# Delta rule stage: filter taps read PSUM, key norms summed on TensorE, key and output scaling moved to VectorE, the block inverse loaded in two parts, decay masks moved off GpSimd

## The reference

```python
qkvz = x @ W_in                                   # 128 -> 4 * 1024
q, k, v, z = jnp.split(qkvz, 4, axis=-1)
b, a = jnp.split(x @ W_ba, 2, axis=-1)
qkv = silu(causal depthwise convolution of q, k, v with 4 taps)
beta = jax.nn.sigmoid(b)
g = -A * jax.nn.softplus(a + dt_bias)
q = _l2norm(q) * HD ** (-0.5)                     # per head, sum of squares over 64
k = _l2norm(k)
def step(S, inp):                                 # over time, per head
    S = S * jnp.exp(gt)[..., None, None]
    pred = jnp.einsum('bhk,bhkv->bhv', kt, S)
    S = S + jnp.einsum('bhk,bhv->bhkv', kt, (vt - pred) * bt[..., None])
    return S, jnp.einsum('bhk,bhkv->bhv', qt, S)
y = y * jax.lax.rsqrt(jnp.mean(y * y, axis=-1, keepdims=True) + 1e-06)
y = norm_w * y * jax.nn.silu(z)
```

## Time and profile before

| | |
|---|---|
| runs, median of 3 | 5853.05 us |
| profiled execution | 5847.35 us, of it the span 5845.6 us |
| PE busy | 4513.3 us, 77% |
| DVE busy | 3523.2 us, 60% |
| POOL busy | 1876.9 us, 32% |
| ACT busy | 1798.5 us, 31% |
| mean granted TensorE clock | 0.771 |

### The profile page before, as it was taken

The page is one execution under the profiler, slowest core; times in us unless marked ns, Lnnn a source line. Parts: engine busy times, 40 slices in busy tenths (PEclk is TensorE's granted clock), DMA queues, the critical chain, the costliest instruction groups (busy, mean ns, idle before and its releaser), DMA issues. The chain is left out here.

```text
span 5845.6 us, 160862 instructions
## 1 busy us (share of the span) xinstructions
PE 4513.3 (77%) x65093; PEld 3139.4 (54%) x65093; DVE 3523.2 (60%) x6479; ACT 1798.5 (31%) x3215; POOL 1876.9 (32%) x2605
## 2 busy tenths in 40 slices
PE   7888869999664788877888788878788876886544
PEld 6666634444332556655666556656556655665221
DVE  3444458887674666666666666666566543554677
ACT  0000011111343344444444444444444422332000
POOL 1111100000452455555555455554454541000000
PEclk6555579999785888888888888888888885555766
DMA  0000000000463121222222222222222110001110
GB/s 13 11 11 11 12 22 14 11 14 9 108 148 96 37 42 40 43 44 44 42 40 43 42 45 43 41 41 44 43 45 42 41 35 17 18 18 46 30 32 25
DMA packets 702651, 219.50 MB, mean 38 GB/s; under 512 B 561624, under 2 KB 676000, under 8 KB 701600
## 3 DMA queue, kind: packets, MB, share of 16 engines
q1 hardware_dynamic: 693536, 205.97, 15.9%
q10 hardware_dynamic: 8448, 4.20, 0.2%
HBM read 123.44 MB, written 86.53 MB: 36 GB/s over the span
## 5 line engine op out<-in xcount | busy, mean ns | idle before, releaser
L1736 DVE SCALAR_TENSOR_TENSOR d_acc<-d_xr,d_cq,d_acc 128x512 f32<-128x512 f32 x768 | 643.3, 838 | 149.5 <-ACT d_acc L1402 127.9
L1558 PE MATMUL d_pa<-d_wv,d_hs 128*128 128x512 f32 x1024 | 603.5, 743 | 1.1 <-issue 1.0
L1378 POOL TENSOR_TENSOR d_prod<-d_tblk,d_ablk 128x15 f32<-128x15 f32 (+7 forms) x960 | 376.5, 392 | 583.3 <-DMA d_ablk<-a_blocks 513.1
L1533 PE MATMUL d_pa<-d_hq,d_wqk 128*128 128x259 f32 x1024 | 388.6, 515 | 79.7 <-ACT d_acc L1402 50.9
L1381 POOL TENSOR_TENSOR d_tblk<-d_tblk,d_prod 128x15 f32<-128x15 f32 (+7 forms) x960 | 386.9, 403 | 75.2
L1558 PEld LDWEIGHTS d_pa<-d_wv,d_hs 128*128 128x128 f32 x1024 | 248.7, 250 | 284.7 <-issue 269.5
L1596 PE MATMUL d_pb<-d_ti,d_at 32*32 32x16 f32 x8192 | 123.8, 207 | 351.1 <-POOL d_ti L1355 310.6
L1401 ACT ACTIVATE d_xr<-d_pa 128x518 f32<-128x518 f32 x256 | 154.0, 601 | 647.2 <-PE d_pa L1533 644.4
L1596 PEld LDWEIGHTS d_pb<-d_ti,d_at 32*32 32x32 f32 x8192 | 116.7, 147 | 377.2 <-issue 376.9
L1533 PEld LDWEIGHTS d_pa<-d_hq,d_wqk 128*128 128x128 f32 x1024 | 224.3, 242 | 140.8 <-issue 105.9
L240 PE MATMUL a_ps<-a_v,a_pr 128*128 128x17 f32 x1024 | 229.4, 376 | 57.7 <-DVE a_pr L314 57.7
(11 more groups left out here) (378 smaller groups left out, 10782.5 us busy)
## 6 DMA issues: line engine op xcount, KB each, us to landing
decays<-g_dec SPq DMA_DIRECT2D x16, 2048.0 KB, 7.4
d_dd<-decays SPq DMA_DIRECT2D x64, 512.0 KB, 3.6
d_hs<-h_t SPq DMA_DIRECT2D x512, 32.0 KB, 2.4
t_blocks<-d_tblk SPq DMA_DIRECT2D x64, 256.0 KB, 2.0
a_blocks<-d_at SPq DMA_DIRECT2D x512, 16.0 KB, 1.7
d_ablk<-a_blocks SPq DMA_DIRECT2D x64, 128.0 KB, 2.1
d_ti<-t_blocks SPq DMA_DIRECT2D x512, 16.0 KB, 1.8
d_tt<-t_blocks SPq DMA_DIRECT2D x512, 16.0 KB, 1.9
```

The source lines that it names most:

```text
L1378: link(pool.tensor_tensor(prod[:, 0:s + 1, 0:n], tblk[:, 0, 0:s + 1, s].unsqueeze(2).to_broadcast([P, s + 1, n]), ablk[:, s, s + 1:SB].uns ...
L1533: last = pe.matmul(pa[:, A + b, 0:QH], wqk[:, col * P:(col + 1) * P], hq[:, n, b, :], start=True, stop=True)
L1558: last = pe.matmul(pa[:, B + m, :], hs[:, u % 2, t, :], wv[:, t, cols(m)], start=(t == 0), stop=(t == TAPS - 1))
L1736: last = dve.scalar_tensor_tensor(out=own, in0=xr[:, e % 2, :, t:t + QT], scalar=cq[:, t, col:col + 1], in1=own, op0=ALU.mult, op1=ALU.add)
```

## The change

- SP: the store of `a_blocks` and the reload of `ablk` move to the head of the iteration, ahead of decays, `hs`, gates and `xt`. The inverse is stored as soon as it stands, its transpose after the copy; 6 reloads for `ti` wait for the first store and for `w5_sum`, 8 for `tt` for the second store and for the solve. `ti` gets a column block of its own for what `w4` reads, and the cleaning falls away.
- POOL: loses the cleaning, the key scaling and the output scaling. The block inverse is built in the other orientation, with as many operations.
- TensorE: a projection writes to `pa`, or for block 1 to `pc`, and waits until the filter that last read that bank is done (`conv_done`). Query transposes go; two groups of eight matmuls sum squares with a 128x2 matrix `of_head`. `w4` stands directly behind `kkq`, and the other groups are shifted by a projection or so.
- ScalarE: no raw copies, no copies of keys and outputs; it squares `kq` directly.
- VectorE: reads taps from PSUM, scales keys and outputs from PSUM, reads norm sums from PSUM instead of reducing.
- Gate stage: VectorE applies the masks, one chunk at a time.

The diff, cut to what the text speaks of:

```diff
-                if have(p, q):
-                    for c in range(2):
-                        pool.wait_ge(sem("decays"), NC * v + 2 * c + 2)
-                        own = dec[:, q % 2, 2 * c:2 * c + 2, :, :].rearrange("p c h t -> p (c h) t")
-                        pool.tensor_tensor(own, own, due[:, :].unsqueeze(1).to_broadcast([P, 2 * DH, CH]), ALU.mult)\
-                            .then_inc(sem("masked"), 1)
...
+                def mask(c):
+                    dve.wait_ge(sem("decays"), NC * v + c + 1)
+                    dve.tensor_tensor(dec[:, q % 2, c, :, :], dec[:, q % 2, c, :, :],
+                                      due[:, :].unsqueeze(1).to_broadcast([P, DH, CH]), ALU.mult).then_inc(sem("masked"), 1)
...
+        def raw(e):
+
+            return pc if e == 1 else pa[:, A:A + 2, :]
...
-                if have(p, u) and have(p, u + 3) and (not isinstance(p, int) or i >= 1):
-                    hold(sem("o_ready"), i)
-                    load_gates((u + 3) % 4, i + 3)
+                if have(p, u + 1):
+                    hold(sem("at_ready"), 2 * (i + 1) + 2)
+                    for n in range(NBLK):
+                        c0 = SB * (n % (CH // SB))
+                        sp.dma_start(a_blocks[n, :, :, :].rearrange("h s t -> s h t"),
+                                     at[SB * n:SB * n + SB, (u + 1) % 2, :, c0:c0 + SB]).then_inc(sem("a_stored"), 16)
+                    hold(sem("a_stored"), 16 * NBLK * (i + 2))
+                    sp.dma_start(ablk[:, :, :], a_blocks.rearrange("n h s t -> (n h) s t")).then_inc(sem("a_loaded"), 16)
                 if have(p, u) and have(p, u + 2):
...
+                if have(p, u) and have(p, u + 3) and (not isinstance(p, int) or i >= 1):
+                    hold(sem("o_ready"), i)
+                    load_gates((u + 3) % 4, i + 3)
...
+                    hold(sem("inverse"), i + 2)
+                    sp.dma_start(t_blocks[0].rearrange("n h r c -> (n h) r c"), tblk[:, 0, :, :]).then_inc(sem("ti_stored"), 16)
                     hold(sem("turned_back"), i + 2)
-                    sp.dma_start(t_blocks.rearrange("n h a r c -> (n h) a r c"), tblk[:, :, :, :])\
-                      .then_inc(sem("t_stored"), 16)
-                    hold(sem("t_stored"), 16 * (i + 2))
+                    sp.dma_start(t_blocks[1].rearrange("n h r c -> (n h) r c"), tblk[:, 1, :, :]).then_inc(sem("tt_stored"), 16)
+                    hold(sem("ti_stored"), 16 * (i + 2))
+                    hold(sem("w5_sum"), i + 1)
+                    for n in range(NBLK):
+                        rows = slice(SB * n, SB * n + SB)
+                        m = n % (CH // SB)
+                        if m != 3:
+                            c1 = SB if m == 1 else HB
+                            sp.dma_start(ti[rows, :, c1:c1 + SB], t_blocks[0, n, :, :, :].rearrange("h r c -> r h c"))\
+                              .then_inc(sem("ti_loaded"), 16)
+                    hold(sem("tt_stored"), 16 * (i + 2))
                     hold(sem("solved"), 2 * (i + 1))
                     for n in range(NBLK):
-                        rows, c0, c1 = slice(SB * n, SB * n + SB), SB * (n % (CH // SB)), SB * (n % (HB // SB))
-                        sp.dma_start(ti[rows, :, c1:c1 + SB], t_blocks[n, :, 1, :, :].rearrange("h r c -> r h c"))\
-                          .then_inc(sem("t_loaded"), 16)
-                        sp.dma_start(tt[rows, :, c0:c0 + SB], t_blocks[n, :, 0, :, :].rearrange("h r c -> r h c"))\
-                          .then_inc(sem("t_loaded"), 16)
+                        rows, c0 = slice(SB * n, SB * n + SB), SB * (n % (CH // SB))
+                        sp.dma_start(tt[rows, :, c0:c0 + SB], t_blocks[1, n, :, :, :].rearrange("h r c -> r h c"))\
+                          .then_inc(sem("tt_loaded"), 16)
...
-                if have(p, u):
-                    pool.wait_ge(sem("t_loaded"), 32 * NBLK * (i + 1))
-                    pool.tensor_tensor(ti[:, :, 0:SB], ti[:, :, 0:SB],
-                                       lo[:, :].unsqueeze(2).to_broadcast([P, DH, SB]), ALU.mult)\
-                        .then_inc(sem("ti_clean"), 1)
...
-                    if kept(u + 1):
-                        slot = (u + 1) % 2
-                        hold(sem("k_taken"), k + 1)
-                        pool.wait_ge(sem("wr_ready"), k + 1)
-                        pool.tensor_tensor(heads(ktok[:, slot, :]), heads(ktok[:, slot, :]), spread(wr[:, :]), ALU.mult)\
-                            .then_inc(sem("kw_ready"), 1)
...
-                if have(p, u) and carried(u):
-                    pool.wait_ge(sem("qs_taken"), carries(p, u))
-                    pool.tensor_tensor(heads(o[:, :]), heads(o[:, :]), spread(gt[:, u % 4, 1, :]), ALU.mult)\
-                        .then_inc(sem("oi_ready"), 1)
...
-                act.activation(xr[:, e % 2, :, :], pa[:, A:A + 2, 0:QH], ACT.Copy).then_inc(sem("x_raw"), 1)
-                act.activation(acc[:, e % 2, :].rearrange("p (b t) -> p b t", b=2), pa[:, A:A + 2, TAPS - 1:QH], ACT.Identity,
+                act.activation(acc[:, e % 2, :].rearrange("p (b t) -> p b t", b=2), raw(e)[:, :, TAPS - 1:QH], ACT.Identity,
...
+            def square(u, kind):
+                n, here = tokens_of(u)
+                act.activation(sqT[:, kind, :, :].rearrange("p j (b t) -> p j b t", b=2), kq[:, n, :, kind, here, :, :],
+                               ACT.Square).then_inc(sem("k_squared" if kind == 0 else "q_squared"), 1)
...
+                    hold(sem("conv_done"), done)
                     if have(p, u + 1):
                         hold(sem("qk_read"), 2 * (NCH * p + u + 1) + 1)
-                hold(sem("x_last"), done)
+                elif e == 1:
+                    if have(p, u) and carried(u):
+                        hold(sem("ks_taken"), carries(p, u))
+                    elif have(p, u):
+                        hold(sem("y_ready"), 2 * (NCH * p + u))
+                    hold(sem("conv_done"), done - CB + 1)
+                else:
+                    hold(sem("conv_done"), done - 1 if e == 2 else done)
                 for b in SEQS:
-                    last = pe.matmul(pa[:, A + b, 0:QH], wqk[:, col * P:(col + 1) * P], hq[:, n, b, :],
+                    last = pe.matmul(raw(e)[:, b, 0:QH], wqk[:, col * P:(col + 1) * P], hq[:, n, b, :],
...
+            def sum_squares(kind):
+                for j in range(DJ):
+                    last = pe.matmul(pb[:, 1, DH * kind + 2 * j:DH * kind + 2 * j + 2], sqT[:, kind, j, :], of_head[:, :],
+                                     start=True, stop=True)
...
-                    conv(p, u, 0)
                 if now:
-                    hold(sem("ti_clean"), i + 1)
+                    hold(sem("ti_loaded"), 16 * 6 * (i + 1))
                     if past:
                         hold(sem("x_used"), i - 1 + X_AHEAD)
                     for h in range(DH):
                         for b, w in BLOCKS:
                             rows = rows_of(b, w)
                             last = pe.matmul(pb[rows, 0, h * SB:(h + 1) * SB], at[rows, u % 2, h, HB * w:HB * w + HB],
-                                             ti[rows, h, 0:SB], start=True, stop=True)
+                                             ti[rows, h, HB:HB + SB], start=True, stop=True)
                     last.then_inc(sem("w4_sum"), 1)
                 if cv:
-                    conv(p, u, 1)
+                    conv(p, u, 0)
...
+                if far:
+                    if now:
+                        hold(sem("tt_ready"), i + 1)
+                    hold(sem("tq_ready"), n)
+                    hold(sem("k_squared"), n + 1)
+                    sum_squares(0).then_inc(sem("k_summed"), 1)
...
-                    turn(u + 2, 1, A).then_inc(sem("q_turned"), 1)
+                    hold(sem("n4_ready"), n + 1)
+                    hold(sem("q_squared"), n + 1)
+                    sum_squares(1).then_inc(sem("q_summed"), 1)
                 if now:
-                    if far:
-                        hold(sem("k_taken"), n + 1)
+                    if far and kept(u + 2):
...
-                    last = dve.scalar_tensor_tensor(out=own, in0=xr[:, e % 2, :, t:t + QT], scalar=cq[:, t, col:col + 1],
+                    last = dve.scalar_tensor_tensor(out=own, in0=raw(e)[:, :, t:t + QT], scalar=cq[:, t, col:col + 1],
...
+                    if kept(u + 2):
+                        dve.wait_ge(sem("k_turned"), keeps(p, u + 2))
+                        if now:
+                            dve.wait_ge(sem("update"), keeps(p, u))
+                        dve.tensor_tensor(heads(ktok[:, u % 2, :]), heads(two(pa, B)), spread(wr[:, :]), ALU.mult)\
+                           .then_inc(sem("kw_ready"), 1)
+                if now and carried(u):
+                    dve.wait_ge(sem("qs"), carries(p, u))
+                    dve.tensor_tensor(by_group(o[:, :]), by_head(pa[:, A:A + 2, :]),
```

(37 more changed lines are left out.)

168 lines of the change are left out of this document (79 added, 89 removed).

## The result

The changed kernel takes 5407 us (median; 5395 to 5420), the kernel before, run beside it, 5857 (5845 to 5861). The ratio is 0.9237 (95% interval 0.9223 to 0.9251): 450 us less, where 293 had been forecast. The range of the prediction (5300 to 5730) holds it; the narrower band that it called the forecast (5450 to 5670) does not. The profiled execution of the changed kernel took 5395.4 us, span 5393.7.

What follows compares the result with a forecast made beforehand. The ring SP, POOL, SP was taken as the bound, 45.5 us a step; then TensorE's path, 32.8 + 2.7 + 0.6 + 5.2 = 41.3. Steps save 284 us, with the gate stage 294: forecast 5560, range 5300 to 5730.

Steps and rivals of the forecast that it cites:

- rival 1: Delta stage: TensorE leads without gaps or clock falls, 36.1 us a step, 5250 us; with the half of it, chance 0.28.
- The ring: Delta stage: the circle SP, POOL, SP through stores and reloads sets the step; it falls from 45.5 to 35.9 us.
- rival 4: SP's queue: a late `at` at its head delays everything behind, the ring isn't shortened; within 0.3%, 5850 us; chance 0.03.
- TensorE's work: Delta stage: 32.8 us a step at full clock, plus net 2.7 for norm sums replacing query transposes.
- Taps: VectorE's 12 filter taps a step, read from PSUM: 838 ns towards 684, saving 0 to 1.8 us, on no path.
- Waits for filters: TensorE in a walked step: projections and output transposes wait for filters to read their banks; 0.6 us, bounds 0 and 3.
- Rival 2: Projection waits some 3 us a step for ScalarE's product and three taps on its bank; 44.3 a step, 5735; chance 0.13.
- Gaps: TensorE's unexplained idle times, 1.8 us a step at today's rate, 2.5 with more gaps in w4.
- Falls of the clock: TensorE slows behind gaps: 3.0 us a fall, 2.6 to 3.5 a step; gaps and falls together 5.2.
- the sign: TensorE's granted clock in a step near 0.91 would show the forecast right.
- The gate stage: Decay masks move from POOL to VectorE, ending its hold-ups: -10 us over 16 units, between -30 and +20.
- Rival 3: Slower: TensorE's clock falls in both norm sums, 3.0 us each; 47.3 a step, 5940 us; chance 0.06.

Runs made afterwards that it cites:

- order-and-split: Kernel before with SP's new order and with ti and tt stored and loaded apart, no cleaning on POOL: 5409 us, ratio 0.9224.
- order, split and masks: Kernel before with SP's new order, ti and tt stored and loaded apart without cleaning, and decay masks on VectorE: 5372 us, ratio 0.9185.
- thinned: Changed kernel with one norm-sum matmul call in place of eight, the other heads' norms left out: 5329 us, ratio 0.9113.

## Why the prediction was right, and where not

**The number.** The range held, the forecast in it did not. A step of 39.1 us and a time of 5407 lie below the band that had 0.50 (39.5 to 43, 5450 to 5670), in the half of rival 1 that had 0.28 (37 to 39.5, 5305 to 5450). Forecast and result differ by 157 us: 120 in the delta stage, most of it the slow clock, and 27 to 40 in the gate stage, on the same side.

**The ring.** Right: 35.9 forecast, 35.6 measured in a turn in which nothing else held SP, and the old order put back restores GpSimd's wait for `ablk`. `at` is late for SP (rival 4) by 3.3 us a step, and it costs GpSimd 1.4 us a step of waiting for `ablk`; since TensorE leads, it costs no time.

**TensorE's work.** Right: 32.8 + 2.7 = 35.5 forecast, 35.2 in a step at full clock; 1.84 us per norm sum on either count. Against the 33.1 us of order-and-split steps at full clock the change adds 2.1 us, not 2.7, and the 32.8 was 0.3 too low: the two errors partly cancel.

**Taps.** 838 against 684 ns was read as the price of the source. It was not, both sources take 0.75 us; the term lay on no path, so the sum did not suffer.

**Waits for filters.** Rival 2 did not come: those for `qk` and `yT` are 0.24 us a step. The 0.5 us for ScalarE's copy of w5 (L1662) had no line in my walk; projection and copy were closer than I read. Together 0.7 for 0.6, right in size but by another mechanism.

**Gaps.** Right in the sum, 2.3 us a step against 1.8 to 2.5, and partly by luck. w4's came as I had it, 68.5 us for 73. But t4's, which I left at 54.2, fell to 15.9, and the loop's start rose from 20.5 to 36.4. w4 had gaps in 49 of 59 steps, and in 22 of 57 with the filter projection ahead of it, so its neighbour counts for something; the place is set by the count of records, which I did not look at.

**Falls of the clock: the term that failed.** I took 3.0 us for each and nearly one a step, 3.0 of the 5.2. It was 0.7 a step. First, price and rate were read from a kernel whose TensorE also waited for the ring: the earlier trace rows show the first two thirds of a fall of some 6.8 us, with three groups in it, and in the changed kernel the median one lasts 3.4 us and the one read costs 1.6. Second, there are fewer: 15 per 1000 us where there were 36, as there are fewer idle stretches over 0.9 us, 25 for 49. These 2.3 us are all of the difference between the 41.3 and the 39.1 us of a step. The granted clock over the stage was 0.95, above the 0.91 that I had named as the sign. As for rival 1, the step without gap or fall that it describes exists, at 36.2 us, and about a third of the steps are near it; the mean lies between it and the forecast.

**The gate stage.** Forecast -10, measured -37 to -50. The hold-ups were about 6 us a unit, not 4 to 5: L991 (2.2 to 2.7 us), L1001 (2.1), and 0.15 us on each of eight larger operations. I charged the four masks (4.9 us a unit) against the end in full, but VectorE's wait for the exponential `eb` (L998) fell from 44.9 to 25.0 us in 250. I take it that part of the masks ran where it had stood; no run separates that.

**Slower.** Rival 3's fall in the norm sums was put at 0.06; in the changed kernel none is shown. Doubled sums, whose falls are mostly of that kind, took back 405 of the 450 us, but even they did not turn the sign.

**What I did not ask.** Whether the other parts are needed at all. By my own steps norm sums add 2.7 us to the engine that leads, and PSUM taps could save time only on engines that do not. The runs say the same: order, split and masks alone are 35 us faster.

**Open.** The falls cost less with norm sums (0.7) than without or thinned (2.0). The total of the gaps (2.3, 2.5 and 3.1 us a step) does not explain that, the number of idle stretches over 0.9 us does in part: 25, 37 and 35 per 1000 us. Norm sums change the count of records and with it where the multiples of 256 fall, so this may be no merit of the sums; no run separates where they stand from how many there are. Why 14 of the 25 stretches, but 27 of the 35, are followed by a fall is open too. PSUM taps, scalings and TensorE's new order were not run each by itself.

## What to carry to other kernels

A DMA queue that serves a ring is a list of issues: what the ring needs goes to its head, what merely has to be ready a step later goes under the longest computation, and this alone, with a load split by who needs it first, was the whole gain in the delta stage. On the engine that leads, a microsecond of waiting or of nearly empty matmuls can cost two, since the clock falls behind it: price the falls from a stretch in which that engine leads, not from one in which it waits. Where gaps have no releaser, number the engine's records before you look for a cause in their neighbours. A mean can hide a tail: look at the median before you put a difference down to where an operand lies. After a change of several parts, run the two that your own sum says carry it; here they beat the whole.

## What the runs showed of the hardware

TensorE's clock fell to 1.2 GHz without idle time just before it, 1.4 us behind 3.6 us of 128x128 matmuls with two columns (row of the granted clock above); 34 of 47 falls in that kernel had a norm sum and no idle stretch over 0.9 us in front of them, none of 15 with half as many such matmuls; 3.63 us more of such work a step cost 6.6. Gaps without a releaser in runs of 32x32 matmuls, 1 to 3 us each, moved to the next such run, rather than go, when long matmuls were put between; within a round of the loop all 595 in fourteen traces stood multiples of 256 TensorE records apart, to within 2. Two wide products a unit on GpSimd lengthened two small VectorE operations to 2.3 to 2.9 us on average where they take 0.17 and 0.23. A tap of 128x512 took 0.75 us from SBUF and from PSUM alike. The same eight DMA issues took from 3.7 to 6.5 us in one kernel.
